# A two-layer gated transformer block on one core: experts in two halves of tokens, result stores on ScalarE, and one closing block in place of two

## The reference, cut to what matters

```
layer 0: x += tanh(g) * cross_attention(layernorm(x), ctx of 64 tokens, 16 heads)
         xt = layernorm(x)
         scores = sigmoid(xt @ gate_w.T);  idx = top 4 of 16 of (scores + gate_b)
         w = 2.5 * scores[idx] / sum(scores[idx])
         y = sum over the 4 experts e of  w_e * (silu(xt @ w1_e.T) * (xt @ w3_e.T)) @ w2_e.T
         x += tanh(g) * (y + the same with shared weights, without routing)
layer 1: x += tanh(g) * causal_attention(layernorm(x), memory = ctx, 16 heads)
         x += tanh(g) * bitlinear(x): layernorm; scale by 128 / max|all of it|; clip; matmul with
              weights rounded to -1, 0, 1 by their mean |w|; scale back
```

## Time and profile before

| what | us |
|---|---|
| three runs | 1500.81, 1505.89, 1510.85 (median 1505.89) |
| the profiled execution, its own time | 1509.58 |
| its span in the trace | 1507.7 |

### The profile page before, as it was taken

One profiled execution on the slowest core, in us unless ns is written; L12 is line 12 of the kernel. 1 busy time (PEld: TensorE's weight loads), 2 busy tenths in 40 slices (PEclk: granted clock), 3 DMA queues, 4 the chain that ended last, 5 costly groups with the idle time before them and its releaser, 6 DMA issues. The chain is left out here.

```text
span 1507.7 us, 23775 instructions
## 1 busy us (share of the span) xinstructions
PE 1099.7 (73%) x8143; PEld 565.5 (38%) x8155; DVE 1012.5 (67%) x1851; ACT 637.0 (42%) x1280; POOL 482.1 (32%) x533
## 2 busy tenths in 40 slices
PE   3799995364019999524645569999999999988857
PEld 2355553232006666312323223333333333331646
DVE  4799985775406766436555478888888888870665
ACT  0446553231003333202212127777777677775430
POOL 1242331777740000277785331111111121111110
PEclk7899996776559999857777659999999999996889
DMA  6101000222749999734576611112111121100003
GB/s 198 34 22 43 30 13 11 81 95 100 269 115 250 248 252 259 214 94 125 174 229 190 173 39 40 39 40 63 52 39 40 49 66 39 39 2 1 1 0 112
DMA packets 183648, 146.23 MB, mean 97 GB/s; under 512 B 102638, under 2 KB 160494, under 8 KB 183546
## 3 DMA queue, kind: packets, MB, share of 16 engines
q1 hardware_dynamic: 162570, 102.61, 25.7%
q0 software_dynamic: 12288, 33.57, 6.8%
q10 hardware_dynamic: 8688, 8.66, 1.8%
HBM read 53.11 MB, written 68.55 MB: 81 GB/s over the span
## 5 line engine op out<-in xcount | busy, mean ns | idle before, releaser
L1801 DVE TENSOR_REDUCE small<-ps 128x2 f32<-128x960 f32 (+6 forms) x384 | 378.9, 1040 | 56.8 <-PE ps L1856 56.5
L1780 ACT ACTIVATE region<-ps 128x512 f32<-128x512 f32 (+5 forms) x768 | 343.1, 532 | 107.8 <-PE ps L1870 106.3
L1751 POOL TENSOR_SCALAR_AFFINE_SELECT region<-region 128x512 f32<-128x512 f32 (+2 forms) x160 | 87.6, 548 | 425.3 <-ACT region L1780 425.2
L1870 PE MATMUL ps<-region 50*128 50x512 f16 (+5 forms) x896 | 197.5, 330 | 27.2 <-ACT region L1780 24.0
L1946 PE MATMUL ps<-region 128*32 128x512 f32 (+5 forms) x1792 | 191.5, 501 | 2.5 <-POOL region L1751 1.9
L1219 PE MATMUL ps<-region 128*128 128x384 f16 x696 | 124.2, 329 | 67.8 <-DMA region<-expert_rows 67.2
L1856 PE MATMUL ps<-region 48*128 48x480 f16 (+6 forms) x896 | 141.4, 333 | 13.5 <-DVE small L1801 11.3
L862 POOL DMA_INDIRECT expert_rows<-region,small x128 | 130.0, 1015 | 51.4 <-issue 38.3
L1384 POOL DMA_INDIRECT region<-result_rows,home x128 | 133.3, 1041 | 38.0 <-issue 36.3
L1870 PEld LDWEIGHTS ps<-region 50*128 50x128 f16 (+1 forms) x896 | 54.2, 94 | 209.8 <-ACT region L1780 195.2
L1219 PEld LDWEIGHTS ps<-region 128*128 x696 | 67.5, 99 | 111.2 <-issue 72.7
(11 more groups left out here) (241 smaller groups left out, 1691.3 us busy)
## 6 DMA issues: line engine op xcount, KB each, us to landing
result_rows<-region SPq DMA_DIRECT2D x58, 384.0 KB, 4.1
region<-v_parts SPq DMA_DIRECT2D x16, 576.0 KB, 4.0
v_parts<-region SPq DMA_DIRECT2D x14, 576.0 KB, 8.6
region<-k_parts SPq DMA_DIRECT2D x96, 68.0 KB, 2.2
region<-q_parts SPq DMA_DIRECT2D x96, 64.0 KB, 2.1
k_parts<-region SPq DMA_DIRECT2D x16, 272.0 KB, 5.0
x_sb<-in_x ACTq DMA_DIRECT2D x8, 512.0 KB, 9.3
region<-in_w13T SPq DMA_DIRECT2D x16, 256.0 KB, 3.0
```

The source lines that it names most:

```text
L1751: nc.gpsimd.affine_select(out=t, in_=t, compare_op=ALU.is_ge, fill=0.0, base=r0, pattern=[[0, G], [1, w]], channel_multiplier=-1).then_inc ...
L1780: nc.scalar.activation(dst, src, ACT.Exp, scale=SCALE).then_inc(s_exp, 1)
L1801: nc.vector.tensor_reduce(nmp[:, qt, :, p0:p0 + np_, place], s_pair(n + first)[:, :, 0:np_ * nk] .rearrange("p e (h k) -> p e h k", h=np_) ...
L1870: ins = nc.tensor.matmul(o, k_of(rr, tbuf)[:, pair, kt * P:kt * P + rows], q_of(rr, tbuf)[:, pair, q0:q0 + nq], start=True, stop=True)
```

## The change

1. The experts' tokens are cut into two halves of 2048 (chunks 0 to 3, 4 to 7). Each half has rows, result rows and tables of its own. GROUP is 256, GROUPS is 47 for each half, so there are 94 groups with 12 matmuls of 256 columns for gate and up and 6 of 256 for down. ROW_BUFS is 6.
2. `tables` of the first half runs after the fourth chunk, ahead of its `add_shared`; `tables` of the second half runs on VectorE within group 1; `homes` at every sixth group from group 5.
3. SP fills the 16 tails of the first half, loads the group registers by fours, and loads groups; it stores no results. ACT stores the result of group g-3 behind silu of group g, and fills one tail of the second half behind groups 6, 8, ... 36. SP loads the weights of the projection block behind group 51, and ACT and VectorE split them at groups 61 and 65.
4. GpSimd, when all rows are sent and all results of the first half are stored, fetches the rows of chunks 0 to 3 into two buffers. VectorE adds them to x behind groups 60 to 91, two instructions per group.
5. The projection block begins with the statistics of chunks 0 to 3 in one go; GpSimd fetches only chunks 4 to 7, and the fetch of chunk c+2 stands behind the power of chunk c.
6. The output and the quantised block become one. Both PARTITION_ALL_REDUCEs go; TensorE sums |w| with a matmul against ones and spreads the maxima with a matmul against the identity matrix. The weights are rounded behind the seventh chunk. TensorE runs 28 spare matmuls (`keep_busy`) around the second of these.

The diff, cut to its core (the tables, buffers and semaphores that only take an index for the half are left out):

```diff
-GROUP = 3 * P
+GROUP = 2 * P
+HALVES = 2
+HALF_TOKENS = B * L // HALVES
-GROUPS = (B * L * TOPK + E * (GROUP - 1)) // GROUP
-ROW_BUFS = 4
+GROUPS = (HALF_TOKENS * TOPK + E * (GROUP - 1)) // GROUP
+ROW_BUFS = 6
-STORE_LAG = 6
+STORE_LAG = 3
+LOAD = 4
...
             def _(sp):
+                def starts(g):
+                    last = min(g + LOAD, (g // GROUPS + 1) * GROUPS)
+                    return list(nc.values_load_multi_w_load_instructions(start_tab[0:1, g:last], ...)[1])
...
+                for e in range(E):
+                    fill_tail(sp, 0, e)
+                for g in range(HALVES * GROUPS):
+                    h = g // GROUPS
+                    if g % GROUPS == 0:
+                        sp.wait_ge(s_tabs, (h + 1) * TABS)
+                    if not first:
+                        first = starts(g)
+                    if g % GROUPS == 0:
+                        sp.wait_ge(s_tail[h], E * 16)
+                        wait_sent(sp, range(h * HC, (h + 1) * HC))
+                    if g >= G_BUFS:
+                        sp.wait_ge(s_ggu, g - G_BUFS + 1)
+                    sp.dma_start_transpose(xgT[:, g % G_BUFS]..., xs[h][bass.ds(first.pop(0), GROUP), :]...)
+                    if g == GROUPS + 4:
+                        for dst, src in ((w_sb[:, :, 0:D], wq1), (w_sb[:, :, D:3 * D], wkv1), (c_sb, ctxT)):
+                            sp.dma_start(dst, ...).then_inc(s_win, 16)
...
             def _(pool):
+                wait_sent(pool, range(CHUNKS))
+                for b in range(Y_BUFS):
+                    pool.wait_ge(s_back[b], len(range(b, GROUPS, Y_BUFS)) * 16)
+                pool.wait_ge(s_homes, HC)
+                for c in range(HC):
+                    if c >= 2:
+                        pool.wait_ge(s_comb, (c - 1) * TC * TOPK)
+                    ... 16 indirect DMAs yg_pair[c % 2] <- ys[0]
...
             def _(act):
+                for g in range(HALVES * GROUPS):
                     silu(g)
+                    if g >= STORE_LAG:
+                        store(g - STORE_LAG)          # waits s_yout, then the DMA
+                    if g == FIRST_TAIL:
+                        act.wait_ge(s_tabs, TABS + 1)
+                    if g >= FIRST_TAIL and g % 2 == 0 and g - FIRST_TAIL < 2 * E:
+                        fill_tail(act, 1, (g - FIRST_TAIL) // 2)
+                    if g == SPLIT_AT:
+                        ... wh, ch <- w_sb, c_sb
...
             def _(dve):
+                for g in range(LAST):
                     group_hidden(g + DEEP - 1); group_out(g); group_hidden_low(g + DEEP - 1)
+                    if g == TABLES_AT:
+                        tables(1)
+                    if g >= HOMES_AT and (g - HOMES_AT) % HOMES_EVERY == 0 and ...:
+                        homes((g - HOMES_AT) // HOMES_EVERY)
+                    if g == SPLIT_LOW_AT:
+                        ... wl, cl
+                    first = (g - GROUPS - COMBINE_AT) * EACH
+                    for n in range(first, first + EACH):
+                        if 0 <= n < HC * TC * TOPK:
+                            combine(n // (TC * TOPK), n % (TC * TOPK))
...
             def _(pe):
-                pe.wait_ge(s_tabs, 3)
+                pe.wait_ge(s_tabs, TABS)
+                pe.wait_ge(s_slot, CHUNKS)
...
 # projection block, GpSimd
+                fetch(FIRST, 0)
+                pool.wait_ge(s_var, 1)
+                nc.gpsimd.tensor_tensor(rstd_first[:], ve_first[:], ..., ALU.pow).then_inc(s_rstd, 1)
+                fetch(FIRST, 1)
+                ...
+                fetch(FIRST + 1, 0)
+                fetch(FIRST + 1, 1)
+                for c in range(FIRST, 2 * B):
+                    rstd_of(c)
+                    if c + 2 < 2 * B:
+                        fetch(c + 2, 0)
+                        fetch(c + 2, 1)
 # projection block, VectorE
+                statistics_first()
                 for c in range(2 * B):
-                    combine(c, 0)
+                    if c >= FIRST:
+                        combine(c, 0)
                     if c:
                         x_low(c - 1)
-                    combine(c, 1)
-                    statistics(c)
+                    if c >= FIRST:
+                        combine(c, 1)
+                        statistics(c)
                     if c:
                         low(c - 1)
                     normalised(c)
...
 # output block, TensorE, behind the last chunk
+                keep_busy(16)
+                eng.wait_ge(s_part, 1)
+                nc.tensor.matmul(gamma_ps, sc1[:, 0:1].to_broadcast([P, P]), ident[:], ...).then_inc(s_gamma, 1)
+                keep_busy(12)
+                for c in range(CHUNKS):
+                    ... the 16 matmuls of each chunk
```

More of the change, by code:

```diff
@@ L792, in flamingo @@
             s_norm, s_pick, s_spare = sem("norm_self"), sem("pick_self"), sem("spare_filled")
-            s_count, s_tabs, s_tself = sem("count"), sem("tables"), sem("table_self")
-            s_tail = sem("tails")
+            s_tabs, s_tself = sem("tables"), sem("table_self")
+            s_tail = [sem(f"tails{h}") for h in range(HALVES)]
+            s_yg, s_comb = [sem(f"token_rows{i}") for i in range(2)], sem("combined")
+            s_win, s_whigh, s_homes = sem("next_weights"), sem("weights_high"), sem("homes")
             s_xg = [sem(f"group{i}") for i in range(G_BUFS)]
@@ L812, in _, with wait_sent @@
+            def wait_sent(eng, chunks):
+                for c in chunks:
+                    eng.wait_ge(s_sent[c % ROW_BUFS], (c // ROW_BUFS + 1) * TC * TOPK * 16)
             @block.sync
             def _(sp):
-                def start(g):
-                    return sp.value_load(start_tab[0:1, g:g + 1], min_val=0, max_val=E * STRIDE)
+                def starts(g):
+                    last = min(g + LOAD, (g // GROUPS + 1) * GROUPS)
+                    return list(nc.values_load_multi_w_load_instructions(start_tab[0:1, g:last], engines=[mybir.EngineType.SP],
+                                                                         min_val=0, max_val=E * STRIDE)[1])
+                first = []
@@ L821, in _ @@
                 sp.wait_ge(s_tabs, 1)
[L822 to L838, removed]
@@ L1091, in _ @@
                         normalised(c + 2)
-                    if c + 1 == CHUNKS:
-                        pick_order.wait()
-                        tables()
-                        for early in range(EARLY):
-                            homes(early)
+                    if c + 1 == HC:
+                        tables(0)
                     add_shared(c)
@@ L1999, in _ @@
             def _(pool):
-                pool.wait_ge(s_wsum, 1)
-                nc.gpsimd.partition_all_reduce(sc1[:, 3:4], sc1[:, 1:2], P, RADD).then_inc(s_wsum, 1)
-                with pool.Fori(0, CHUNKS) as c:
+                nc.gpsimd.memset(onesf[:], 1.0).then_inc(s_ones, 1)
+                for c in range(CHUNKS):
                     ln_pool(nc.gpsimd, c, s_var, s_rstd)
+            @block.sync
+            def _(sp):
+                for c in range(CHUNKS):
+                    sp.wait_ge(s_added, c + 1)
+                    sp.dma_start(out[c * CH:(c + 1) * CH, :].rearrange("(t p) d -> p t d", p=P),
+                                 x_sb[:, c * TC:(c + 1) * TC, :]).then_inc(s_out, 16)
+                sp.wait_ge(s_out, CHUNKS * 16)
             @block.scalar
@@ L2116, in body, with keep_busy @@
                     transposes(rg, period, (f"x0{h}", f"x1{h}"), c)
+                def keep_busy(n):
+                    for _ in range(n):
+                        nc.tensor.matmul(spare_ps, onesf[:], ident[:], start=True, stop=True)
                 project(ring_first, 0, 0, 0)
+                eng.wait_ge(s_ones, 1)
+                eng.wait_ge(s_wsum, 1)
+                nc.tensor.matmul(beta_ps, onesf[:], sc1[:, 1:2], start=True, stop=True).then_inc(s_beta, 1)
                 chunks(eng, body)
```

385 lines of the change are left out of this document (215 added, 170 removed).

## The result

The changed kernel takes 1505.84 us, median of 20 runs (1470.34 to 1516.11), the kernel before 1507.22 in the runs taken beside it. By these medians they are 1.4 us apart. The changed kernel's runs spread over 46 us, those of the kernel before over 14. The ratio, 0.9862 [0.9824, 0.9900], rests on the fastest 4 of the 20, since the comparison leaves out runs far above a kernel's fastest. The forecast was 1413. The profiled execution lies near the upper end with 1511.24 us (span 1509.5).

What follows compares the result with a forecast made beforehand. Bounds: GpSimd's sends before the groups, TensorE and DMA both full in them, result fetches in the projection block. 1509.6 - (630.4 - 616) - (223.3 - 152) - 7 = 1417, less 3.7: 1413 us, range 1375 to 1455.

Steps and rivals of the forecast that it cites:

- The groups start: End of routing: groups begin at 377 in place of 445.5, bounds 370 to 385, gain 68 us.
- The projection block: Projection after the groups: 152 us in place of 223.3, low 135, high 190, gain 71 us.
- First scaling: End of kernel: scaling follows the last maximum by 2 to 3 us, now 6.9; gain 4.5 us.
- the end gains: Output and quantised block: 4.5 us after the maximum, 2 from spare matmuls, total 7, between 3 and 10.
- rival 2: Second half's groups: fetches slow down beside busy VectorE, 38 us more, 1451; chance 0.10.
- rival 3: Projection block: fetch and power interlock on GpSimd, last four chunks keep 27.9 us each, 41 us more, 1454; chance 0.07.
- How long 94 groups take: Group loop: four limits priced, TensorE, ScalarE, DMA engines and GpSimd; end at 612, between 591 and 640.
- I take 2.1 with the seam: Group loop, TensorE: matmuls of 256 columns give a 2.1 us period, 197 us for 94 groups, end at 574.
- 1.9, just inside 2.1: Group loop, ScalarE: 1.3 us plus 0.58 for a store; 2.6 with tails, 16 us over TensorE's pace.
- DMA engines: Group loop: 192 us of groups plus 55 us of added traffic, 247 at share 1.0, 227 at 1.09; end 604 to 624.
- They start when the first half is stored: Group loop, GpSimd: 64 fetches at 1.34 us, 86 us, from 500 to 586; groups then end at 607.
- Rival 4: Group loop: period does not shrink with the group, end at 730, 1527; decides from 3.5 us; chance 0.03.

Runs made afterwards that it cites:

- no_fetch: Changed kernel without the 64 fetches of the first half's results beside the groups and without their additions, registers still by fours: 1454.5 us (0.9642).
- reg_ahead_no_fetch: Changed kernel, registers loaded singly, TensorE's unchecked and behind the gate-up matmuls, without the first half's fetches and additions: 1419.3 us (0.9436).
- after_sp_stores: Changed kernel with one edit: results stored from SP, six groups behind, in place of ScalarE: 1455.9 us (0.9649).
- load1_no_fetch: Changed kernel with group registers loaded one at a time on TensorE and SP, without the first half's fetches and additions: 1447.1 us (0.9609).

## Why the prediction was wrong

Four of its steps held. The groups start at 374.6 (377, bounds 370 to 385). The projection block takes 148.3 us (152), its first normalising starts 15.5 us after the block (20, bounds 11 to 36). First scaling comes 2.53 us after the last maximum (2 to 3), the end gains 4.3 + 2.0 us (4.5 + 2). A fetch starts every 1.25 us (1.34), so rival 2 is out; the block is far under 180, so rival 3 is.

The step that failed is "How long 94 groups take": forecast 235 us, measured 335. With the rest right, that alone is the miss: 96.5 us later at the projection block, less 3.7 there. Its four terms:

- TensorE, "I take 2.1 with the seam". The matmuls were right: 1.97, though the 0.113 us per matmul was read from the row of the weight loads (PEld). The register load by fours was in the change and got no price at all. It stands in TensorE's queue, and the 23 periods that hold it last 4.83 us. Made single, unchecked and moved, with the fetches out of the way (no_fetch against reg_ahead_no_fetch), it is worth 35 us.
- ScalarE, "1.9, just inside 2.1", and 2.6 with tails. ScalarE was priced as an engine, 0.58 us for a store. It never was the limit. What its stores cost is 50 us (after_sp_stores; 32 by the ratios), more than half of it as TensorE's waits for loads that land late, 14 us as busy time of TensorE at a lower granted clock.
- DMA engines, 247 us at a share of 1, 227 at 1.09. The prices came from windows in which one kind of transfer ran alone, and were added as if the sum of engine time were kept when they mix. The fetches got 23 us and cost 51 with their additions (33 by the ratios). The bandwidth at a given share falls where three queues meet: 172 GB/s at 1.13 from 545 to 603, 250 at 1.07 with the stores on SP. The rule of the Trainium skill (DMA: Bandwidth & Descriptors, "Issuing engines are not separate DMA queues") that several starters save issue time alone held in that the stores on ScalarE bought no bandwidth; the runs go further: beside the fetches they cost some.
- GpSimd, "They start when the first half is stored", at 500: 544.9, and the last at 671.1 in place of 586, since both follow the groups.

Rival 4 had the nearest time, 1527, and its turning point, a period of 3.5 us, was right: 335 / 94 = 3.57, and the kernel is no faster in this execution. Its reason was not: an undisturbed group shrank to 1.97, two thirds of 2.93. What added up were periods of 3 to 10.6 us at a part of the groups. The range missed because both of its ends took stores and fetches at their quiet prices and the register loads at none.

These costs do not add. One at a time they are worth at most 15 (registers), 50 (stores) and 51 us (fetches), and the registers 35 once the fetches are out: whichever limit is lifted, the next one stands just behind. TensorE alone needs 2.0 us per group, and the quiet stretch of reg_ahead_no_fetch still takes 2.37.

What stays open is why the engines lose time when three queues meet: that they do is shown, the cause inside them is not. Nor was the number of load buffers varied: a load can start only when the gate-up matmuls four groups back are done, and in the jams loads land up to 23.4 us after their start. With more buffers the same slow loads might cost less.

## What to carry to other kernels

A DMA share near or above 1 says that packets are under way, not that bytes arrive; read GB/s beside it, and how early loads land. Prices from windows with one kind of transfer added up to the time of the kernel before and were far too low for this mix, so measure the mix before stores get a queue of their own beside loads and GpSimd's transfers. A register load stands in its engine's own queue: put it, singly, behind enough issued work to cover it, and look at what then waits behind it.

## What the runs showed of the hardware

A register load's price differs from place to place. Four at once take 1.41 us, one in front of the gate-up matmuls 0.56 (load1_no_fetch), one behind them, unchecked, 0.31 (reg_ahead_no_fetch): medians of TensorE's queue, bounds checks not counted.

Loads slow down per packet. The DMA queues from 560 to 600, first in the changed kernel, then in after_sp_stores (q1 is SP's queue, q10 ScalarE's, q0 GpSimd's: packets, MB, share of 16 engines):

```profile
q1 hardware_dynamic: 6642, 1.65, 54.9%
q0 software_dynamic: 1251, 3.39, 44.8%
q10 hardware_dynamic: 1776, 1.70, 15.8%
```

```profile
q1 hardware_dynamic: 18670, 7.39, 79.2%
q0 software_dynamic: 985, 2.67, 23.9%
```

In the changed kernel SP's queue holds loads alone: 0.549 x 16 x 40 us / 6642 = 53 ns per packet. In reg_ahead_no_fetch, with stores on ScalarE and no fetches, the same window gives it this row:

```profile
q1 hardware_dynamic: 19108, 4.75, 75.9%
```

That is 25 ns. A packet of GpSimd's takes 0.448 x 640 / 1251 = 229 ns in the jam, and 155 where loads and stores share a queue. So in the jam a load's packet takes some twice as long and GpSimd's half as long again, and a share of 1.16 moves 169 GB/s where after_sp_stores moves 253 at 1.04.

The Trainium skill (DMA: Bandwidth & Descriptors, "Queues, rings and completion order") says that each engine takes packets in turn from the queues that have work. By that, if its packets are those of the profile, a load's small packets get one turn in three beside a queue of stores and GpSimd's, one in two where they share the stores' queue. The runs agree in direction; that the packets themselves take longer is more than the rule says, and no run here separates the two.
